# Channel sums of a spatial attention map: turned and added in 32x32 blocks on VectorE instead of summed by matmuls on TensorE

## What is computed

```python
# x: 8 x 256 x 160 x 160
ll, lh, hl, hh = haar_dwt(x)                                   # each 8 x 256 x 80 x 80
fused = relu(bn(conv1x1(concatenate([ll, lh, hl, hh], axis=1), fusion_w, fusion_b)))
avg_sp = mean(fused, axis=1, keepdims=True)                    # over the 256 channels
max_sp = max(fused, axis=1, keepdims=True)
sp_map = conv7x7(concatenate([avg_sp, max_sp], axis=1), sa_w)  # padding 3, one output channel
spatial_out = sigmoid(sp_map) * fused
avg_ch = mean(spatial_out, axis=(2, 3)); max_ch = max(spatial_out, axis=(2, 3))
ch_map = sigmoid(mlp(avg_ch) + mlp(max_ch))
projected = relu(bn(conv1x1(ch_map * spatial_out, proj_w, proj_b)))   # 1024 channels
out = haar_idwt(projected's four quarters) + x
```

## Time and profile before

| | |
|---|---|
| median of 3 runs | 2567.86 us |
| runs | 2569.47, 2567.86, 2566.55 us |
| the profiled execution | 2566.07 us |
| its span, first to last instruction | 2564.3 us |
| granted TensorE clock, mean (1 is 2.4 GHz) | 0.987 |
| PE, PEld, DVE, ACT, POOL busy | 95, 83, 81, 42, 15% of the span |
| DMA queues | q1 50.1%, q0 36.5% of 16 engines' span |

### The profile page before, as it was taken

How to read it: one execution, slowest core, us unless ns; L and a number is a source line. 1 busy time by engine, 2 the same in 40 slices (tenths; PEclk the granted TensorE clock), 3 DMA queues, 4 the chain that set the end, 5 groups by cost and what they waited for, 6 DMA issues and landing times. The chain is left out here.

```text
span 2564.3 us, 32151 instructions
## 1 busy us (share of the span) xinstructions
PE 2429.5 (95%) x12373; PEld 2121.6 (83%) x12373; DVE 2066.0 (81%) x2611; ACT 1072.1 (42%) x1421; POOL 388.1 (15%) x347
## 2 busy tenths in 40 slices
PE   5999999999999999999999999999999999986886
PEld 4888889898898978888898888989888888975765
DVE  4756778797778887788787987788877888779898
ACT  3444534354344533455334543445434453324222
POOL 0010111111111111111111111111111111122233
PEclk9999999999999999999999999999999999988999
DMA  4445699999999999999999999999999999886687
GB/s 142 159 159 178 183 279 273 269 294 262 253 276 272 294 254 258 281 273 285 261 265 271 287 271 271 270 274 292 256 260 268 281 291 258 232 286 243 247 289 281
DMA packets 110301, 660.26 MB, mean 257 GB/s; under 512 B 15362, under 2 KB 16452, under 8 KB 109892
## 3 DMA queue, kind: packets, MB, share of 16 engines
q1 hardware_dynamic: 83940, 487.80, 50.1%
q0 software_dynamic: 26208, 170.41, 36.5%
HBM read 448.04 MB, written 210.12 MB: 257 GB/s over the span
## 5 line engine op out<-in xcount | busy, mean ns | idle before, releaser
L483 PE MATMUL pp<-y_hi,wp_hi 128*128 128x480 f32 (+1 forms) x1792 | 677.4, 378 | 75.5 <-DVE y_lo L824 45.2
L746 DVE TENSOR_TENSOR x_lo<-xin,x_hi 128x1920 fp32r<-128x1920 f32 (+1 forms) x224 | 461.9, 2063 | 318.9 <-ACT x_hi L576 318.8
L576 ACT ACTIVATE x_hi<-xin 128x1920 fp32r<-128x1920 f32 (+1 forms) x224 | 418.1, 1867 | 671.1 <-PE pf L497 671.1
L497 PE MATMUL pf<-x_hi,wf_hi 128*128 128x480 f32 (+1 forms) x1792 | 677.7, 378 | 11.3 <-DVE wp_lo L741 6.2
L483 PE MATMUL pp<-y_lo,wp_hi 128*128 128x480 f32 (+1 forms) x1792 | 671.0, 374 | 0.0
L483 PE MATMUL pp<-y_hi,wp_lo 128*128 128x480 f32 (+1 forms) x1792 | 668.6, 373 | 0.0
L497 PE MATMUL pf<-x_hi,wf_lo 128*128 128x480 f32 (+1 forms) x1792 | 665.3, 371 | 0.0
L497 PE MATMUL pf<-x_lo,wf_hi 128*128 128x480 f32 (+1 forms) x1792 | 664.7, 371 | 0.0
L483 PEld LDWEIGHTS pp<-y_hi,wp_hi 128*128 128x128 f32 x1792 | 341.6, 191 | 133.9 <-DVE y_lo L824 61.1
L606 ACT ACTIVATE relu<-pp,t 128x480 f32<-128x480 f32 (+1 forms) x448 | 285.1, 640 | 397.3 <-PE pp L483 357.2
L801 DVE SCALAR_TENSOR_TENSOR xre<-sd,both 128x960 f32<-128x960 f32 (+1 forms) x364 | 410.3, 1169 | 6.5
(11 more groups left out here) (89 smaller groups left out, 1180.7 us busy)
## 6 DMA issues: line engine op xcount, KB each, us to landing
xin<-in_x_dram SPq DMA_DIRECT2D x160, 960.0 KB, 6.7
out_dram<-xre SPq DMA_DIRECT2D x160, 960.0 KB, 5.2
xre<-in_x_dram POOLq DMA_DIRECT2D x130, 960.0 KB, 9.3
xin<-in_x_dram SPq DMA_DIRECT2D x64, 800.0 KB, 6.5
out_dram<-xre SPq DMA_DIRECT2D x64, 800.0 KB, 4.5
xre<-in_x_dram POOLq DMA_DIRECT2D x52, 800.0 KB, 8.9
xre<-in_x_dram SPq DMA_DIRECT2D x30, 960.0 KB, 6.6
sigb<-sig_scratch SPq DMA_DIRECT2D x56, 400.0 KB, 7.9
```

Source lines behind the costliest of these rows:

```text
L483: mm = pe.matmul(pp[j][:, 0:n_px], w[:, kt, cols], y[:, s.pc, kt, 0:n_px], start=(kt == 0 and m == 0), stop=(kt == CT - 1 and m == 2))
L497: mm = pe.matmul(pf[o][:, 0:n_px].rearrange("p (y w) -> p y w", w=W2), w[:, i, q, o * P:(o + 1) * P], v[:, q % 2, :, q // 2, :], start=(i ...
L576: nc.scalar.activation(halves(x_hi, i, k), pairs(i, k), ACT.Copy).then_inc(xhi_ready[i], 1)
L746: nc.vector.tensor_tensor(halves(x_lo, i, k), pairs(i, k), halves(x_hi, i, k).bitcast(F32), ALU.subtract).then_inc(xlo_ready[i], 1)
```

## The change

The sums take the way of the maxima. POOL's `channel_sum` stays, but over the blocks of the tile, as `span_of` gives them (up to 480 points, some from a block's start in the row before). In the slot in which `sm` is made, DVE turns it in 32 x 32 blocks and reduces it by addition into `blocksum` (`turn_sums`), behind `y_lo` and ahead of the first gate and the maxima. In phase 0 PE turns both `blocksum` and `blockmax` (four transposes), DVE reduces both (`spatial_maps`) into `across_all`, which lies in `sigb`, and SP stores both maps and loads both with one DMA. The matmuls with `pick`, and ACT's copy of the sums, go; the factor 1/256 is put into the convolution's taps once at the start.

```diff
-    map_dram = nc.dram_tensor("map_scratch", [1, NPX], F32, kind="Internal").ap()
+    map_dram = nc.dram_tensor("map_scratch", [2, NPX], F32, kind="Internal").ap()
...
+        across_all = sigb[0:NPX // GROUP // 2, 0:4 * GROUP].rearrange("p (m h j) -> p m h j", m=2, h=2)
+        turned_sum = sd[:, 0, PXM:2 * PXM]
...
                 if s.phase == 0:
-                    sp.wait_ge(maxima_ready, s.nb + 1)
-                    sp.dma_start(map_dram.rearrange("o (h p j) -> (o p) h j", h=2, j=GROUP), maxima[:, :, :]
-                                 ).then_inc(map_stored, 16)
+                    sp.wait_ge(across_ready, 2 * (s.nb + 1))
+                    for m in range(2):
+                        sp.dma_start(map_dram[m:m + 1, :].rearrange("o (h p j) -> (o p) h j", h=2, j=GROUP),
+                                     across_all[:, m, :, :]).then_inc(map_stored, 16)
...
-                    sp.dma_start(maps[:, 1, PAD:PAD + W2], map_dram.rearrange("o (h w) -> (o h) w", w=W2)
+                    sp.dma_start(maps[:, :, PAD:PAD + W2], map_dram.rearrange("m (h w) -> h m w", w=W2)
                                  ).then_inc(map_landed, 16)
...
             def channel_sum(s):
                 k = s.k - 1
-                n = px_of(k)
+                block, px, n = span_of(k)
+                here = ring_px(k // TILES, px, n)
                 gp.wait_ge(f_ready, CT * (k + 1))
                 if s.load_next:
                     gp.wait_ge(xlo_ready[0], s.k + 2)
-                need(gp, sum_psum, k)
-                nc.gpsimd.tensor_tensor(sm[:, 0:n], fused[:, 0, ring(k)], fused[:, 1, ring(k)],
+                need(gp, sum_turned, k)
+                nc.gpsimd.tensor_tensor(sm[:, 0:n], fused[:, 0, here], fused[:, 1, here],
                                         ALU.add).then_inc(sm_ready, 1)
...
-            def add_channels(s):
-
-                k = s.k - 1
-                pe.wait_ge(sm_ready, k + 1)
-                if s.phase == 1:
-                    pe.wait_ge(mean_ready, s.nb + 1)
-                for r in range(ROWS[k % TILES]):
-                    row = FIRST[k % TILES] + r
-                    at, base = row % GROUP, row - row % GROUP
-                    m = min(GROUP, H2 - base)
-                    mm = pe.matmul(sums[base:base + m, :], pick[:, GROUP - 1 - at:GROUP - 1 - at + m],
-                                   sm[:, r * W2:(r + 1) * W2], start=(at == 0), stop=(at == m - 1))
-                mm.then_inc(sum_psum, 1)
...
                 if s.phase == 0:
                     pe.wait_ge(blockmax_ready, s.k)
-                    for h in range(2):
-                        n = NPX // GROUP // 2
-                        mm = pe.transpose(across[:, h * P:(h + 1) * P], blockmax[:, h * n:(h + 1) * n], ident[:, :])
+                    pe.wait_ge(blocksum_ready, s.k)
+                    for to, blocks in ((across_sum, blocksum), (across, blockmax)):
+                        for h in range(2):
+                            n = NPX // GROUP // 2
+                            mm = pe.transpose(to[:, h * P:(h + 1) * P], blocks[:, h * n:(h + 1) * n], ident[:, :])
                     mm.then_inc(across_psum, 1)
...
-                if s.turn:
-                    add_channels(s)
...
-                if s.phase == 1:
-                    act.wait_ge(sum_psum, s.k - 1)
-                    need(act, conv_psum, s.nb)
-                    nc.scalar.activation(maps[:, 0, PAD:PAD + W2], sums, ACT.Copy, scale=1.0 / C
-                                         ).then_inc(mean_ready, 1)
...
+            def turn_sums(s):
+
+                block, px, n = span_of(s.k - 1)
+                blocks = -(-n // GROUP)
+                dve.wait_ge(sm_ready, s.k)
+                if s.c:
+                    need(dve, cell_ready, 4 * s.kc if s.phase == LAST else 4 * s.kc + 2)
+                need(dve, blocksum_ready, s.k - 1)
+                nc.vector.transpose(turned_sum[:, 0:blocks * GROUP], sm[:, 0:blocks * GROUP]).then_inc(sum_turned, 1)
+                dve.wait_ge(sum_turned, s.k)
+                need(dve, across_psum, (s.k - 1) // TILES)
+                nc.vector.tensor_reduce(blocksum[:, block:block + blocks],
+                                        turned_sum[:, 0:blocks * GROUP].rearrange("p (n c) -> p n c", c=GROUP),
+                                        AX.X, ALU.add).then_inc(blocksum_ready, 1)
...
+            def spatial_maps(s):
 
                 dve.wait_ge(across_psum, s.nb + 1)
-                need(dve, map_stored, 16 * s.nb)
-                nc.vector.tensor_reduce(maxima[:, :, :],
-                                        across.rearrange("p (h a j) -> p h j a", h=2, j=GROUP),
-                                        AX.X, ALU.max).then_inc(maxima_ready, 1)
+                need(dve, mult_done, CT * NCH * s.nb)
+                for m, (groups, op) in enumerate(((across_sum, ALU.add), (across, ALU.max))):
+                    nc.vector.tensor_reduce(across_all[:, m, :, :],
+                                            groups.rearrange("p (h a j) -> p h j a", h=2, j=GROUP),
+                                            AX.X, op).then_inc(across_ready, 1)
...
+                if s.turn:
+                    turn_sums(s)
                 if s.phase in GATED:
                     gate(s, GATED[s.phase][0])
...
             dve.wait_ge(taps_landed, 16)
+            nc.vector.tensor_scalar(taps[:, 0:KS * KS], taps[:, 0:KS * KS], 1.0 / C, None, ALU.mult
+                                    ).then_inc(taps_ready, 1)
+            dve.wait_ge(taps_ready, 1)
```

More of the change, by code:

```diff
@@ L118, in haar_block @@
         ident = sb("ident", [P, P])
-        pick = sb("pick", [P, 2 * GROUP - 1])
         blockmax = sb("blockmax", [P, NPX // GROUP])
-        maxima = sb("maxima", [NPX // GROUP // 2, 2, GROUP])
+        blocksum = sb("blocksum", [P, NPX // GROUP])
         squeeze = sb("squeeze", [P, CT, HID])
@@ L165, in haar_block @@
         pm = ctx.enter_context(nc.psum_tensor("pm", [P, 1024], F32))
-        sums = pm[0:H2, 0:W2]
+        across_sum = pm[0:NPX // GROUP // 2, 0:2 * P]
         conv = pm[0:H2, 512:512 + W2]
@@ L195, in haar_block @@
         bias_ready = sem("bias_ready")
+        taps_ready = sem("taps_ready")
         band_pass = sem("band_pass")
@@ L208, in haar_block @@
         sm_ready = sem("sm_ready")
-        sum_psum = sem("sum_psum")
+        sum_turned = sem("sum_turned")
+        blocksum_ready = sem("blocksum_ready")
         across_psum = sem("across_psum")
-        mean_ready = sem("mean_ready")
-        maxima_ready = sem("maxima_ready")
+        across_ready = sem("across_ready")
         map_stored = sem("map_stored")
@@ L267, in plain_upto, with span_of @@
             return sum(not adding(*divmod(n, 2)) for n in range(g + 1))
+        def span_of(k):
+            t = k % TILES
+            block = FIRST[t] * W2 // GROUP
+            return block, block * GROUP, (FIRST[t] + ROWS[t]) * W2 - block * GROUP
         def uses(g, by_dma):
@@ L359, in body @@
                 if s.phase == 0:
-                    sp.wait_ge(map_stored, 16 * (s.nb + 1))
+                    sp.wait_ge(map_stored, 32 * (s.nb + 1))
                     need(sp, conv_psum, s.nb)
-                    sp.dma_start(maps[:, 1, PAD:PAD + W2], map_dram.rearrange("o (h w) -> (o h) w", w=W2)
+                    sp.dma_start(maps[:, :, PAD:PAD + W2], map_dram.rearrange("m (h w) -> h m w", w=W2)
                                  ).then_inc(map_landed, 16)
@@ L386, in _ @@
             nc.gpsimd.memset(maps[:, :, :], 0.0).then_inc(ones_ready, 1)
-            nc.gpsimd.memset(pick[:, :], 0.0).then_inc(pool_mem, 1)
-            gp.wait_ge(pool_mem, 3)
-            nc.gpsimd.memset(pick[:, GROUP - 1:GROUP], 1.0).then_inc(ones_ready, 1)
+            gp.wait_ge(pool_mem, 2)
             nc.gpsimd.affine_select(out=ident[:, :], in_=ident[:, :], compare_op=ALU.not_equal, fill=1.0,
@@ L469, in _ @@
             pe.wait_ge(wflo_ready, 4)
-            pe.wait_ge(ones_ready, 2)
+            pe.wait_ge(ones_ready, 1)
             def project(s, i):
@@ L772, in butterflies @@
                     dve.wait_ge(blockmax_ready, s.k + 1)
+                if s.turn and (i == 1 or s.phase == LAST):
+                    dve.wait_ge(blocksum_ready, s.k)
                 for n, j in enumerate((LL, HL)):
@@ L826, in lower @@
                                                    ALU.mult, ALU.subtract).then_inc(lo_ready, 1)
-            def span_of(k):
-                t = k % TILES
-                block = FIRST[t] * W2 // GROUP
-                return block, block * GROUP, (FIRST[t] + ROWS[t]) * W2 - block * GROUP
             def channel_max(s):
@@ L854, in turn @@
                                         AX.X, ALU.max).then_inc(blockmax_ready, 1)
-            def spatial_max(s):
-                dve.wait_ge(across_psum, s.nb + 1)
-                need(dve, map_stored, 16 * s.nb)
-                nc.vector.tensor_reduce(maxima[:, :, :],
```

(9 more changed lines are left out.)

1 line of the change is left out of this document (removed).

## The result

The changed kernel takes 2505.62 us (median of 4 runs, 2504.51 to 2508.07) where the kernel before takes 2568.66 us (2566.55 to 2572.24) in the same comparison: ratio 0.9755, 95% interval 0.9741 to 0.977. It is faster by 63 us; the forecast was 2515 us, a gain of 53, with a range of 2478 to 2548. The profiled execution took 2504.5 us, its span 2502.4, at a mean granted clock of 0.982.

The account below looks back on a forecast made before the run. PE was taken to be the limit nearly everywhere. Ungated slots 56 us gained, gated 5 lost, start 4 gained, last image 1 and clock 1 lost: 53 us, so 2513 us against the median 2515, range 2478 to 2548.

Parts of the forecast that it names:

- Steady slots: Ungated slots, images 1 to 7: 21.0 us instead of 22.14, pair hidden in DVE's waits; 67 us gained, 56 net of phase 0.
- Phase 0: PE's turns wait some 1.6 us for the pair behind y_lo, plus 0.3 for more turns: 11 us lost over six slots.
- The start: Slots 0 to 20, no projection: 7 us gained in slots 8 to 13, less phase 0 and gated losses; net 4 gained.
- for slots 1 to 7 ... nothing: Start, where the bands fill the rest: the ring shrinks by 0.2 us at most, so no gain.
- The gated slots: Phases 2 to 6, images 2 to 7: PE's 5.6 us saving becomes waits, y_lo 0.8 us later an image; 5 us lost.
- DVE is the limit: Gated slots: with the pair DVE's round takes 22.3 us where PE needs 21.0, so DVE sets the slot.
- The ring that I put at 22.3 us: Gated slots: DVE's round from x_lo back to x_lo, 22.07 us before, with the pair added.
- The last image: PE's turns wait 6 us for the pair behind y_lo, but PE stands idle 4.68 us later anyway; 1 us lost.
- DVE's lateness does not reach PE: Rival, chance 0.12: DVE has unseen slack, so the gated slots give their 34 us; 2476 us.
- DMA as the limit: Rival, chance 0.15: 21.5 us of packets in a steady slot, so 61 slots give 0.5 us less each; 2546 us.
- The pairs cost more than their twins: Rival, chance 0.07: POOL contention or semaphore waits add 0.5 us on 112 slots beyond the maxima's pairs; 2540 to 2572 us.
- The fall of the clock: Rival, chance 0.06: PE's clock falls in the gated slots of six images, 75 us lost, kernel slower; 2590 us.

Follow-up runs that it names:

- the early pair: Changed kernel with the phase 0 transpose and reduction of the sums ahead of y_lo instead of behind it: 2502.04 us, ratio 0.9732.
- the experiment on it: Kernel with two sigb buffers, phase 0 pair ahead of y_lo and gated pairs moved to phases 8 to 12, plus slot 112's pair at the slot's head: 2481.33 us.
- two buffers: Changed kernel with two buffers for the sigmoid map's chunks (second in cell), each load issued one chunk ahead: 2497.84 us.
- both: Changed kernel with two sigb buffers and the pairs of phases 2 to 6, images 2 to 7, left out: 2492.24 us.
- the last kernel: Kernel with two sigb buffers, moved gated pairs and earlier pairs (phase 0, slot 112), plus ScalarE's sums writing to cell, not relu: 2451.07 us, ratio 0.9541.

## Why the prediction was right, and where it was not

**Steady slots: right, and shown.** 21.00 us for 22.14; the pair vanished in DVE's waits; it could even be made twice. With phase 0 and phase 7 the stretch gave 56.5 us for 56 (60 of the 61 slots are in it).

**Phase 0: the mechanism was right, the size near.** 1.19 us of wait a time where I said 1.6, and the early pair took it away (6.4 us of six slots).

**The start: mis-sized, 9.9 us for 4.** The term "for slots 1 to 7 ... nothing" failed. I took DVE and POOL for the limit of those slots. Before, they took 82.0 us. PE's fusion and pick matmuls are 10.5 + 1.15 us in five of them and 8.75 + 1.0 in two, 77.8 in all, and 4.0 us of waits for POOL's sum are the rest: PE was busy or held by its own pick matmuls throughout. Now they take 77.8 us and PE waits 4.9 us for `x_lo`; without pairs 74.2. So 4.2 us were gained there, until a new wait stopped it. The rest of the miss lies in slots 14 to 20: 2.8 us of loss were forecast, and they took 85.5 us before and 85.4 now. Slots 8 to 13 gave 6.7 us for 7. Against this stand 1.2 us that slot 1 starts later, which is no more than its scatter (59.4 to 61.5 us in the changed kernel and its variants).

**The gated slots: the size near (-1.7 for -5), the reason only a third of it.** "DVE is the limit" was true in the sense that DVE has no wait in phases 2 to 4 of images 2 and 4. The ring that I put at 22.3 us runs in 22.12 without a wait, from one `x_lo` to the other in the timeline of DVE of the changed kernel, image 2:

```profile
493.56 2.15 DVE L736 TENSOR_TENSOR x_lo<-xin,x_hi 128x1920 fp32r<-128x1920 f32 x1
...
501.78 0.67 DVE L850 STREAM_TRANSPOSE sd<-sm 128x480 f32<-128x480 f32 x1
502.49 0.65 DVE L853 TENSOR_REDUCE blocksum<-sd 128x15 f32<-128x480 f32 x1
503.06 0.98 DVE L809 CUSTOM_DVE_ANT_0 fused<-fused,sigb 128x800 f32<-128x800 f32 x1
...
515.68 1.82 DVE L736 TENSOR_TENSOR x_lo<-xin,x_hi 128x1600 fp32r<-128x1600 f32 x1
```

The pair was priced too high: behind `y_lo` it takes 1.28 us and not 1.4 (the 1.45 of its twin holds 0.09 us in which DVE stood still), and DVE's busy time in phases 2 to 6 rose by 5.9 to 6.2 us and not by 6.9, which leaves nearly nothing of the 0.8 us an image; what was lost is within the scatter that the loads of `sigb` make. PE's wait for `y_lo` in phase 7 is 2.7 or 1.2 us where I said 3.6. But from "DVE is the limit" I drew that without the pair's load on DVE 34 us would be there, the upper bound of this term and the rival's 2476 us. Nothing was: the run without these pairs gained 0. Three rounds lay within 1 us of each other: DVE's own with the pair (phase 3 takes 21.78 us), the load of the single `sigb` (21.4 us, the estimate above), and the ring through ScalarE's sums (21.74 us with no pair). I had the row of the third in hand, DVE's 1.14 us wait for `x_hi`, and booked it as slack that a pair may fill. The pair did fill it, which is why it cost so little. But a wait that each round repeats is also the mark of another chain as long as the engine's own; I subtracted it from the ring of 22.07 and never asked what makes `x_hi` late.

**The last image: -2.8 for -1.** PE waits 6.32 us for `blocksum` there, as expected; the experiment on it left its price open. The difference itself is no larger than the scatter: four variants whose last image is unchanged (pairs left out of the gated slots, pairs doubled, two buffers, both) take 321.9 to 325.3 us for this stretch.

**The rivals.** "DVE's lateness does not reach PE" fell with its 34 us, as told above. DMA as the limit fell: with the DMA share at 0.98 steady slots are 21.00 us, and with 1.02 and 314 GB/s phases 2 and 3 of the last kernel are too. "The pairs cost more than their twins" fell: 112 pairs cost 17 us in all, 8 of them in phase 0. The fall of the clock came, but small. In the timeline of PE of the changed kernel, image 3:

```profile
840.29 0.42 PE L507 MATMUL pf<-x_hi,wf_hi 128*128 128x400 f32 x1 [2.29 <-ACT fused L648]
```

and the stretch that follows it, in the columns of the stretches above:

```profile
841.60:845.00 3.40, 3.40 (x13) 3.37 (x12) 3.29 (x6) 1.59 (x3) 0.00 (x0) 0.50 1.04 270
```

Shortly after a wait of 2.29 us PE ran at half clock (1.2 GHz) for 3.4 us. Between the start and the last image this happened five times, in images 3, 6 and 7, at a price of at most 1.7 us each; before the change it happened three times there. The Trainium skill, "TensorE: Matmul & The Clock Gate", section "Why this matters for your kernels", warns of gaps between bursts of matmuls. The trace agrees only in part: the waits just ahead of the five pieces were 1.5 to 2.7 us, but a wait of 2.71 us in image 4 had no such piece behind it, and the clock in the stretch after it is 1.00:

```profile
1170.87 0.48 PE L493 MATMUL pp<-y_hi,wp_hi 128*128 128x480 f32 x1 [2.71 <-DVE y_lo L816]
```

```profile
1170.90:1176.00 5.10, 5.10 (x24) 4.41 (x25) 3.75 (x4) 4.47 (x6) 0.00 (x0) 1.00 0.91 274
```

The other page that I weighed, the Trainium skill's "Perfetto Trace Analysis", section "Identifying the Most-Contended Engine", judges TensorE's headroom by the busy share of its weight loads, beside the share of its peak arithmetic, which I did not weigh. By the weight loads DVE (88%) now stands above PE (82%), and one would take work off DVE first. The runs speak against that here: 112 pairs less (122 us of DVE's busy time) bring 17 us, 42 pairs more leave the steady slots at 951.3 us, and a steady slot has PE at its end with weight loads at 18.03 of 21.00 us.
